# Sixteen heads of causal attention with a feed-forward: jobs spread over the units' slots, and low features over 64 rows

## The reference

```python
xn = layernorm(x)
q, k, v = split(xn @ w_qkv.T + b_qkv)              # 16 heads of 16 channels
att = q @ k.T / sqrt(16) + bias[head, i - j]       # bias from cos/sin of the distance, per head
att = softmax(where(causal, att, -inf)); a = att @ v
y = fp8(xn / s_in) @ fp8(kernel / s_k) * (s_in * s_k) + bias   # in bfloat16
out = x + a @ w_proj.T + b_proj + y
```

## Time and profile before

| | |
|---|---|
| median of 3 timed runs | 960.95 us (957.75 to 961.32) |
| the profiled execution's own time | 952.14 us |
| its span, first to last instruction | 950.4 us |
| mean granted TensorE clock | 0.892 |
| TensorE busy | 841.5 us (89%) |
| VectorE busy | 710.5 us (75%) |
| ScalarE busy | 588.9 us (62%) |
| GpSimd busy | 517.1 us (54%) |

### The profile page before, as it was taken

One profiled execution on the slowest core, in us unless ns is written; L12 is line 12 of the kernel. 1 busy time (PEld: TensorE's weight loads), 2 busy tenths in 40 slices (PEclk: granted clock), 3 DMA queues, 4 the chain that ended last, 5 costly groups with the idle time before them and its releaser, 6 DMA issues.

```text
span 950.4 us, 22868 instructions
## 1 busy us (share of the span) xinstructions
PE 841.5 (89%) x6121; PEld 524.2 (55%) x6121; DVE 710.5 (75%) x2523; ACT 588.9 (62%) x1194; POOL 517.1 (54%) x521
## 2 busy tenths in 40 slices
PE   6789898999999999999999999899998989989883
PEld 4456555565555556455565556556555655656442
DVE  4777878887777877777787787878778787887802
ACT  4246757775755666565676666667566666766551
POOL 5433656556645755555555655655565565565550
PEclk9668989999888989788899888989889898999977
DMA  5934566555546654645655545665554566555402
GB/s 146 179 66 87 101 147 120 127 107 137 96 99 126 121 122 86 142 81 112 140 102 124 101 110 110 123 136 97 133 100 113 111 121 141 97 111 100 103 13 75
DMA packets 55549, 106.08 MB, mean 112 GB/s; under 512 B 10464, under 2 KB 30432, under 8 KB 55520
## 3 DMA queue, kind: packets, MB, share of 16 engines
q1 hardware_dynamic: 55048, 105.19, 53.2%
q10 hardware_dynamic: 472, 0.54, 0.2%
HBM read 18.68 MB, written 8.91 MB: 29 GB/s over the span
## 4 chain that ended last, share of the span: by engine, by line
PE 53%; DVE 14%; issue 13%; ACT 7%; SPq 5%; DMA 5%; DVEq 1%; ACTq 1%; POOL 0%; POOLq 0%
PE misc_a L646 16%; PE misc_a L535 9%; PE misc_b L535 6%; PE scoreT_b L624 4%; PE scoreT_a L624 4%; DVE row_max_parts L969 3%; PE score_c L601 3%; ACT probs L879 3%; DVE row_max L957 3%; PE score_a L601 3%; PE scoreT_c L624 3%; SPq L324 2%; DVE score_c L957 2%; PE score_b L601 2%; SPq L372 1%
## 5 line engine op out<-in xcount | busy, mean ns | idle before, releaser
L1174 POOL TENSOR_SCALAR_AFFINE_SELECT probs<-probs 128x512 f32<-128x512 f32 x256 | 159.9, 637 | 375.5 <-ACT probs L879 374.3
L957 DVE CUSTOM_DVE_ANT_0 score_b<-score_b,causal_mask_q 128x384 f32<-128x384 f32 (+3 forms) x321 | 161.8, 521 | 114.8 <-PE score_b L601 114.8
L646 PE MATMUL misc_a<-probs,v_ones 128*32 128x512 f32 (+3 forms) x2048 | 203.1, 550 | 0.4 <-POOL probs L1174 0.4
L957 DVE CUSTOM_DVE_ANT_0 score_a<-score_a,causal_mask_q 128x512 f32<-128x512 f32 x319 | 173.0, 559 | 4.9 <-PE score_b L601 3.2
L957 DVE CUSTOM_DVE_ANT_0 score_c<-score_c,causal_mask_q 128x256 f32<-128x256 f32 (+3 forms) x384 | 170.2, 470 | 2.4 <-PE score_c L601 2.3
L879 ACT ACTIVATE probs<-scoreT_b 128x384 f32<-128x384 f32 (+1 forms) x256 | 133.8, 523 | 58.2 <-PE scoreT_b L624 42.9
L879 ACT ACTIVATE probs<-scoreT_a 128x512 f32<-128x512 f32 (+1 forms) x256 | 141.6, 553 | 28.6 <-PE scoreT_a L624 12.8
L646 PEld LDWEIGHTS misc_a<-probs,v_ones 128*32 128x32 f32 x2048 | 69.6, 131 | 136.8 <-issue 121.6
L879 ACT ACTIVATE probs<-scoreT_c 128x384 f32<-128x384 f32 (+1 forms) x256 | 134.7, 526 | 13.2 <-PE scoreT_c L627 9.7
L957 DVE DVE_READ_ACCUMULATOR2_ANT row_max<- 128x1 f32 x1024 | 142.0, 139 | 0.0
L624 PE MATMUL scoreT_a<-stacks 64*128 64x512 f32 (+3 forms) x320 | 117.0, 385 | 27.8 <-DMA stacks<-neg_max_T 15.6
(11 more groups left out here) (228 smaller groups left out, 1902.7 us busy)
## 6 DMA issues: line engine op xcount, KB each, us to landing
stacks<-qk_parts SPq DMA_DIRECT2D x128, 512.0 KB, 8.2
x_ring<-in_L_attn_x SPq DMA_DIRECT2D x16, 512.0 KB, 3.5
attn<-out_T SPq DMA_DIRECT2D x64, 128.0 KB, 3.8
xn<-recips SPq DMA_DIRECT2D x31, 256.0 KB
out<-x_ring SPq DMA_DIRECT2D x15, 512.0 KB, 3.0
stacks<-neg_max_T SPq DMA_DIRECT2D x128, 4.0 KB
low_features<-neg_max_T SPq DMA_DIRECT2D x124, 4.0 KB
low_features<-probs SPq DMA_DIRECT2D x8, 128.0 KB, 4.4
```

The lines of the kernel that those rows point to most:

```text
L646: last = mm(bank[32 * i:32 * i + 32, P * j:T], VA[:, j, HU * g + i, :, :].rearrange("p d a -> p (d a)"), probs(g, j)[:, i, :], start=(j == ...
L957: last = V.tensor_tensor_reduce(bank, bank, CMQ[:, T - w:T], 1.0, LEAST, ALU.add, ALU.max, MX[:, g % 2, h, qt:qt + 1])
L1174: last = GP.affine_select(out=d, in_=d, compare_op=ALU.is_ge, fill=0.0, base=0, pattern=[[0, HU], [1, P]], channel_multiplier=-1)
```

## The change

The low-feature matmuls go over all 64 rows of their half instead of 34. For that the first side of `EXT` is set to 0 at the start, ahead of the second side's 1, so the additional 30 rows add 0 x 1; SyncE waits for both. The two q/k jobs of a unit, which stood together at slot 8, stand at slots 6 and 9; V's two at slots 6 and 9 instead of both at 6; the projection's at slots 0 and 6 of the fourth unit instead of both at 6. The feed-forward's two jobs move from slot 9 of the third unit to its slot 0. The tables of the copies follow, some of VectorE's and ScalarE's other work moves by a slot or two, and GpSimd's two additions of biases change places. By the order of the tables the PSUM banks of some jobs change too.

```diff
-EXTRA = 34
-QK_AT = [(0, 8), (0, 8), (1, 8), (1, 8)]
-V_AT = [(2, 6), (2, 6)]
-FF_AT = [(2, 9), (2, 9)]
-PJ_AT = [(3, 6), (3, 6)]
+QK_AT = [(0, 6), (0, 9), (1, 6), (1, 9)]
+V_AT = [(2, 6), (2, 9)]
+FF_AT = [(2, 0), (2, 0)]
+PJ_AT = [(3, 0), (3, 6)]
...
-QK_HI_AT, QK_LO_AT = [(0, 8), (0, 8), (1, 8), (1, 8)], [(0, 8), (0, 9), (1, 8), (1, 9)]
-V_OUT_AT = [(2, 6), (2, 6)]
-AH_AT = [(2, 3), (2, 3)]
-FF_OUT_AT = [(2, 9), (2, 10)]
-RESULT_AT = [(3, 6), (3, 8)]
-NORM_AT = [(3, 2), (3, 3), (3, 5), (3, 6)]
+QK_HI_AT, QK_LO_AT = [(0, 6), (0, 9), (1, 6), (1, 9)], [(0, 7), (0, 10), (1, 7), (1, 10)]
+V_OUT_AT = [(2, 6), (2, 9)]
+AH_AT = [(2, 2), (2, 3)]
+FF_OUT_AT = [(2, 0), (2, 1)]
+RESULT_AT = [(3, 1), (3, 7)]
+NORM_AT = [(3, 1), (3, 3), (3, 4), (3, 6)]
...
-STATS_AT, AGGR_AT = [(1, 3), (1, 4), (1, 7), (1, 8)], (1, 10)
-MAGIC_AT = [(2, 3), (2, 5), (2, 6)]
+STATS_AT, AGGR_AT = [(1, 2), (1, 3), (1, 5), (1, 8)], (1, 9)
+MAGIC_AT = [(2, 2), (2, 3), (2, 5)]
...
-            sp.wait_ge(consts_made, 1)
+            sp.wait_ge(consts_made, 2)
...
-                extra = slice(rows.start, rows.start + EXTRA)
...
-                        last = mm(bank, EXT[extra, u, 1, P * j:P * j + P], EXT[extra, u, 0, P * j:T],
+                        last = mm(bank, EXT[rows, u, 1, P * j:P * j + P], EXT[rows, u, 0, P * j:T],
                                   start=False, stop=True)
...
-            pe.wait_ge(consts_made, 2)
+            pe.wait_ge(consts_made, 3)
...
+            GP.memset(EXT[:, :, 0, :].bitcast(F32), 0.0).then_inc(consts_made, 1)
             GP.memset(EXT[:, :, 1, :].bitcast(F32), 1.0).then_inc(consts_made, 1)
...
                     if g == 3:
-                        ffn_bias(b)
+                        add_bias(b)
                     mask(b, g, 0)
...
                     mask(b, g, 1)
                     if g == 2:
-                        add_bias(b)
+                        ffn_bias(b)
```

## The result

The change took the kernel from 961.13 us (four runs, 957.75 to 965.12) to **898.01 us** (four runs, 896.9 to 899.42): a ratio of 0.9376, 95% interval 0.9331 to 0.942. The profiled execution took 896.9 us with a span of 895.1, against a span of 950.4. The forecast of 906 with a range of 885 to 942 held the time. The steps behind it did not all hold.

What follows compares the result with a forecast made beforehand. TensorE, busy 89% at mean clock 0.892, sets the pace. Per batch: clock -2.7, waits -1.4, entries +0.8, net -3.3 us; -46 over 14 batches, -2 for first and last: 952.1 to 904, plus 2 gives 906 us, range 885 to 942.

Steps and rivals of the forecast that it cites:

- Its own signs: Expected marks: mean clock 0.95 or more, 1.00 in the third head, no L543 wait, quarters near 14, 13, 13, 12.5 us.
- The reading that working rows count, not only busy time: TensorE's heads: the clock falls where only a small part of the array works for a few microseconds; an inference.
- the rows bring nothing: Rival, low-feature matmuls: clock goes by busy time, only third and fourth quarters return; 917, or 919 with 2 added; chance 0.18.
- the first two quarters: Batch stretches up to the second unit's slot 3: clock excess of 0.4 and 1.0 us, of which 0.3 and 0.5 return.
- 1.8 us of clock at the third head: Second-to-third-unit quarter: feed-forward in the third head returns the whole 1.8 us clock excess a batch; bounds 0 and 1.8.
- I take 0; bounds 0 and 1 us a batch: SyncE's queue: third unit's row maxima land no later, although q/k's second low part is written one slot later.
- in the rivals, with 0.11: Rival, SyncE's queue: next stack and third unit's row maxima leave later, a wait takes the place; 928 to 932; chance 0.11.
- +0.8 for entries into full-array work: Split q/k, V and projection pairs: four more entries and exits at 0.2 us cost 0.8 us a batch; bounds 0.4 and 1.0.
- the lower bound of 0.7: Second input transpose (L543 before): the 1.0 us wait for the second projection result goes; bounds 0.7 and 1.0.
- The low-part wait: End of the fourth unit's head: first projection job covers the row maxima's low-part wait, 0.4 us a batch; bounds 0 and 0.6.
- the 0 to 14 ns of the 64-row form: Low-feature matmuls: 64 rows cost 0 to 14 ns more each, at most 0.4 us a batch; taken as 0.
- the swap of the bias additions: GpSimd: two additions of 2.14 and 2.37 us change places at no cost; if fully busy, fourth head begins 0.2 us later.

Runs made afterwards that it cites:

- The pair with 64 and 34 rows: Changed kernel with the third unit's row maxima sent ahead of the regrouping on SyncE's queue, low features over 64 rows (864.58 us) or 34 (884.65 us).
- Moving one line: Changed kernel with the third unit's row maxima sent ahead of the first unit's output regrouping on SyncE's queue: 864.58 us, ratio 0.9028.
- the fastest version: Changed kernel with the row maxima sent ahead of the regrouping for the first, third and fourth unit's heads: 861.11 us, ratio 0.9004.
- a fourth of the same kind: Changed kernel with row maxima ahead of the regrouping at all four heads, including the exchange across the batch: 904.73 us, ratio 0.9471.

## Why the prediction was right, and which of its steps were not

The total of 906 is 8 us above the measured 898. It is a sum of errors in both directions, and its closeness is in part luck. A batch takes 3.8 us less (55.5 to 51.7), forecast were 3.3. Of these, 1.5 is the clock that the first, second and fourth quarter lost before. Another 1.8 is that these three are shorter at full clock for the same work: 36.5 us against 39.3, of which 1.0 is work that moved to the third. The last 0.5 is the third quarter, which takes 0.5 longer with 1.0 more work. The forecast had it the other way round: 2.7 from the clock and 0.6 from all else. Its own signs show that too: a mean clock of 0.95 or more (0.928 came), 1.00 in the third head (0.89 in its quarter), and quarters near 14, 13, 13 and 12.5 us (12.9, 12.0, 15.2 and 11.6).

**Right: what lowers the clock.** The reading that working rows count, not only busy time, was an inference from two heads. The pair with 64 and 34 rows shows it; the rival "the rows bring nothing" falls for the split jobs. The Trainium skill ("TensorE: Matmul & The Clock Gate", Part 1) ties the clock to how busy the engine has been. By that rule the two kernels of the pair, with 0.55 us idle each in that quarter, would have the same clock, and the measured 0.88 and 1.00 decide against it as a full account.

**Too small: the first two quarters.** I took 0.3 of 0.4 us and 0.5 of 1.0 as returned. Both came back whole: the clock falls in none of 13 batches, where it fell in 7 and 9. In the second neither part does it alone: with 34 rows it falls in 7 batches, with q/k in pairs in 11, with 64 rows in the kernel before in 9.

**The failed term: 1.8 us of clock at the third head.** It was counted as returned wholly. Hardly any of it was: the clock falls in the quarter in all 13 batches (12 before), and against the 12.0 us that it takes once the wait is cut it loses 3.2, of which 1.6 is busy time at the lower clock (it was 1.9 before, 13.54 less 11.61) and 1.6 idle time. The step that failed was the one on SyncE's queue, "I take 0; bounds 0 and 1 us a batch". The wait grew by 20.3 us in sum, and at the third head by 1.3 a batch, above the bound. It was in the rivals, with 0.11. Two things were overlooked. As long as a transfer lands no sooner, the wait for it grows by what the waiting engine gains ahead of it, so it couldn't stay at 1.1 with the forecast's own gains in place. And the feed-forward was to fill the head, but it stands behind slot 0, that is behind the wait; the sum counted wait and clock as two separate terms, and here the one brings the other. Moving one line brings both back.

**The wrong sign: +0.8 for entries into full-array work.** Splitting the jobs saves instead: of the 1.8 us that three quarters are shorter at full clock, the two waits below are 1.0, so 0.8 is saved where 0.8 was charged. At full clock the second quarter went from 12.6 to 12.0, and with q/k in pairs it is 12.6 again. TensorE's idle time in that quarter falls from 0.85 us (12.6 less 11.75 busy) to 0.51, and its busy time from 11.75 to 11.49. So the double block had cost idle time, which I had set to 0, and the extra pitches of 0.12 us don't show in the quarter's busy time at all. Which engine's copies made the difference no run separates.

**Waits: nearly.** L542 still waits 0.4 us each of the 1.0, so 0.6 was saved, below the lower bound of 0.7. The low-part wait fell from 10.8 us to 4.4 in the entries for `misc_a` and `misc_b` together. In the kernel before, the transposes behind the fourth and the first unit's heads read, in batch 2:

```profile
149.82 0.28 PE L585 MATMUL misc_b<-ident_f,row_max_parts 128*32 128x128 f32 x1 [0.37 <-DVE row_max_parts L969]
164.89 0.28 PE L585 MATMUL misc_b<-ident_f,row_max_parts 128*32 128x128 f32 x1 [1.28 <-DVE xnT_lo L939]
```

The first of these waits, 0.36 to 0.38 us in each of 13 batches, is gone in the changed kernel (0.2 us for the projection's result are left in 3 batches), so the 0.4 was gained as forecast. The second, for the normalised input's low part, stood in 6 of the 13 batches, those in which the clock had not fallen in that quarter, and stands in all 13 now: 16.7 us in sum against 8.5. Part of what the clock returns in the first quarter is lost to it.

**Nothing, as forecast:** the memset and the 0 to 14 ns of the 64-row form. The second clear ends at 6.2 us, and the first reciprocal deviation starts at 7.21 us (8.18 before), after 0.90 us of waiting for VectorE's statistics. With the clock at 1.00 the second quarter's busy time is 11.49 us for the same matmuls (11.75 before). No run tries the swap of the bias additions by itself.

**The parts are not additive.** Taken out of the changed kernel one at a time they cost 0.7% (rows, not resolved), 1.6% (feed-forward), 2.2% (q/k) and 3.0% (projection) of the time before: 7.5% in sum, where all together bring 6.2%. With the third head's wait cut, rows and feed-forward cost 2.1% and 2.3% of the time before: what a head gets back depends on whether the others hold it down.

**What stays open.** Whether the 64 rows by themselves gain anything in the kernel before. How much of VectorE's time around L968 is GpSimd's doing (below). Why the projection's pair costs most of all the parts: the wait at L542, 0.6 us a batch, is some 8 of its 28 us, and its fourth quarter takes 11.5 us (11.6 with the job of 1.5 us in it) for a reason that no run shows. In the fastest version 18.5 us of waits for VectorE's row maxima and the 1.3 us a batch for the normalised input's low part remain; no run tried them.

## What to carry to other kernels

Where the clock falls, look at how many rows of the array the matmuls use, not only at idle time: zero rows that make a 34-row matmul a 64-row one were worth 20 us here, once the jobs were split and the wait was cut, and a full-array job in a head that had none was worth 22. Before you place it, look at what the stretch waits for: behind a wait of about 2 us the same job was worth some 12 us instead of 22, and a wait for a transfer that lands no sooner grows by whatever the engine gains ahead of it. On a queue in program order, send first what the bounding engine waits for, but follow the transfer that is put back to its own reader: one exchange was worth 33 us, a fourth of the same kind cost 44.

## What the runs showed of the hardware that was not expected

- **Issuing a transfer takes longer when the queue is loaded.** On SyncE the regrouping of the denominators takes 0.63 to 0.66 us to issue 9 to 10 us behind the last stack, and 2.05 where the stack's two transfers left 5 us earlier; the four small ones of the row maxima take 2.72 us behind the regroupings and 5.14 directly behind the stack. The small transfers land 10.0 us after the stack's issue with nothing else between.
- **A lower clock with TensorE busy for 96% of a stretch.** 13.15 of 13.70 us busy at 0.88, 13.04 of 13.60 at 0.87 (with the slower matmuls counted in; at full clock the first stretch is 11.45 of 12.00, 95%); in the first the low features had 34 rows, in the second the head had no full-array job.
- **A 16-column operation of VectorE takes anything from 0.16 to 2.4 us.** In the kernel before, VectorE's timeline shows for the row maxima's low part:

```profile
147.53 2.17 DVE L969 TENSOR_TENSOR row_max_parts<-row_max,row_max_parts 128x16 fp32r<-128x16 f32 x1
...
161.80 1.82 DVE L969 TENSOR_TENSOR row_max_parts<-row_max,row_max_parts 128x16 fp32r<-128x16 f32 x1
```

These two lie beside operations of GpSimd on two inputs and end with them: L1180 runs from 147.53 to 149.67, L1162 from 161.21 to 163.59, and the two above end at 149.70 and 163.62. That the one holds up the other was only seen side by side, not tried.
